# A second buffer for transposed attention blocks, laid over the space of the layer normalisation

## What is computed

```
def _cross_attention(q_in, kv_in, ...):
    qh = (q_in @ wq + bq).reshape(b, q_len, H, K)
    kh = (kv_in @ wk + bk).reshape(b, t, H, K)
    vh = (kv_in @ wv + bv).reshape(b, t, H, K)
    kh = concatenate([kh, bias_k], axis=1)      # one learned row more
    vh = concatenate([vh, bias_v], axis=1)
    weights = softmax(einsum('bqhk,bthk->bhqt', qh, kh) / sqrt(K))
    ctx = einsum('bhqt,bthk->bqhk', weights, vh).reshape(b, q_len, H * K)
    return ctx @ wo + bo

x = x + cross_attention(layer_norm(x), context)     # layer 1
x = x + cross_attention(layer_norm(x), context)     # layer 2
x = x + gelu(layer_norm(x) @ w_fc1 + b_fc1) @ w_fc2 + b_fc2
```

## Time and profile before

| | us |
|---|---|
| median of three runs | 630.03 |
| the profiled execution | 630.57 |
| its span, first to last instruction | 628.8 |
| TensorE busy | 527.1 (84%) |
| VectorE busy | 417.3 (66%) |
| GpSimd busy | 391.0 (62%) |
| ScalarE busy | 341.7 (54%) |
| mean granted clock of TensorE, share of full speed | 0.964 |

### The profile page before, as it was taken

The page is one execution under the profiler, slowest core; times in us unless marked ns, Lnnn a source line. Parts: engine busy times, 40 slices in busy tenths (PEclk is TensorE's granted clock), DMA queues, the critical chain, the costliest instruction groups (busy, mean ns, idle before and its releaser), DMA issues.

```text
span 628.8 us, 10915 instructions
## 1 busy us (share of the span) xinstructions
PE 527.1 (84%) x3217; PEld 456.6 (73%) x3217; DVE 417.3 (66%) x864; ACT 341.7 (54%) x715; POOL 391.0 (62%) x358
## 2 busy tenths in 40 slices
PE   7985888879696989889984896979889897968787
PEld 5865767768585868778863785868777776858787
DVE  3967657575767677665785557677675757566684
ACT  3463746556464847465364464748375655647422
POOL 3736648485857668485744658667584858575830
PEclk9987999999999989899988899999899999999889
DMA  7323424352433434240403533434343424320100
GB/s 230 101 67 76 122 72 121 75 138 67 119 98 79 117 75 121 72 123 13 88 18 75 130 80 104 102 75 121 75 121 75 129 67 135 82 71 15 35 0 35
DMA packets 47909, 55.31 MB, mean 88 GB/s; under 512 B 8698, under 2 KB 33422, under 8 KB 47886
## 3 DMA queue, kind: packets, MB, share of 16 engines
q1 hardware_dynamic: 47886, 55.03, 33.6%
HBM read 25.11 MB, written 0.52 MB: 41 GB/s over the span
## 4 chain that ended last, share of the span: by engine, by line
SPq 39%; DVE 18%; PE 14%; DMA 10%; issue 10%; ACT 5%; POOL 1%; DVEq 0%; ACTq 0%; POOLq 0%
SPq L246 39%; PE ring L998 8%; DVE blocks L727 8%; DMA wf_lo<-blocks 5%; DMA wf_hi<-blocks 4%; ACT probs L557 4%; PE acc L998 3%; DVE total L764 3%; DVE row_max L755 2%; DVE v_sum L712 1%; POOL probs L372 1%; PE ps_ctx L998 1%; DVE z_sb L791 1%; DMA probs<-ctx_in 1%; DVE o_lo L748 1%
## 5 line engine op out<-in xcount | busy, mean ns | idle before, releaser
L365 POOL TENSOR_TENSOR v_lo<-v_sum,v_hi 128x512 fp32r<-128x512 f32 x64 | 85.4, 1337 | 67.7 <-ACT v_hi L515 67.6
L727 DVE STREAM_TRANSPOSE blocks<-probs 128x512 f32<-128x512 f32 x112 | 72.2, 685 | 81.8 <-DMA wf_hi<-blocks 81.8
L557 ACT ACTIVATE probs<-ring,shift 128x512 f32<-128x512 f32 x112 | 76.0, 679 | 52.4 <-DVE shift L760 52.4
L998 PE MATMUL ring<-k_lo,q_hi 128*128 128x512 f32 x112 | 48.2, 431 | 39.7 <-DVE k_lo L697 34.8
L998 PE MATMUL ring<-pT_lo,v_hi 128*128 128x256 f32 x240 | 70.0, 292 | 8.0 <-DVE v_sum L712 8.0
L755 DVE TENSOR_REDUCE row_max<-ring 128x1 f32<-128x512 f32 x112 | 74.2, 681 | 3.3 <-PE ring L998 3.2
L377 POOL TENSOR_TENSOR pT_lo<-wf_lo,pT_hi 128x1024 fp32r<-128x1024 f32 x28 | 67.3, 2404 | 6.5 <-ACT pT_hi L532 6.4
L764 DVE TENSOR_TENSOR total<-row_sum,p_learned 128x2 f32<-128x2 f32 x64 | 31.0, 484 | 59.8 <-ACT probs L557 59.6
L998 PE MATMUL ring<-pT_hi,v_lo 128*128 128x256 f32 x240 | 68.5, 285 | 0.0
L998 PE MATMUL ring<-pT_hi,v_hi 128*128 128x256 f32 x240 | 68.0, 283 | 0.0
L515 ACT ACTIVATE v_hi<-v_sum 128x512 fp32r<-128x512 f32 x64 | 40.1, 629 | 43.2 <-DVE v_sum L712 43.2
(11 more groups left out here) (170 smaller groups left out, 1717.5 us busy)
## 6 DMA issues: line engine op xcount, KB each, us to landing
wf_hi<-blocks SPq DMA_DIRECT2D x224, 64.0 KB, 2.0
wf_lo<-blocks SPq DMA_DIRECT2D x224, 64.0 KB, 2.0
wk_raw<-wk_in SPq DMA_DIRECT2D x17, 256.0 KB, 5.9
wq_raw<-wq_in SPq DMA_DIRECT2D x17, 256.0 KB, 3.0
wv_raw<-wv_in SPq DMA_DIRECT2D x16, 256.0 KB, 3.1
vrows<-vrows_in SPq DMA_DIRECT2D x16, 256.0 KB, 6.2
wo_raw<-wo_in SPq DMA_DIRECT2D x16, 256.0 KB, 6.0
wf_raw<-wf_in SPq DMA_DIRECT2D x6, 256.0 KB, 2.7
```

Source lines behind the costliest of these rows:

```text
L365: pool.tensor_tensor(v_lo[:, 2 * m:2 * m + 2, :], v_sum[:, m % 2, :].rearrange("p (t c) -> p t c", c=PW), v_hi[:, 2 * m:2 * m + 2, :].bitc ...
L557: act.activation(probs[:, u, q, :], ring[S_BANKS[where][QTB * u + q]][:], ACT.Exp, bias=shift[:, u, q:q + 1], scale=SCALE, accum_out=row_s ...
L727: last = dve.transpose(blocks[:, :, u % 2, :, q, :].rearrange("p g c b -> p c g b"), probs[:, u, q, :].rearrange("p (c g b) -> p c g b", g ...
L998: ins = pe.matmul(out_ap, a, b, start=start and i == 0, stop=stop and i == len(passes) - 1)
```

## The change

`z_sb` and `h_full` become two views of one tile, `norm_space`. `blocks` becomes a list of two buffers of 8 KB: a tile of its own for units 0 and 1, and the whole of `norm_space` for units 2 and 3. `move` reads the buffer of its batch. `transpose_blocks` writes the buffer of its batch and waits for the landing of the same move of the step before; in the first step of layer 1 (the first that the kernel runs) it does not wait for a landing at all. No instruction is added or taken away on any engine, and their order stays.

```diff
-        z_sb = sb("z_sb", [P, QT, D])
-        h_full = sb("h_full", [P, DC, TOK])
+        norm_space = sb("norm_space", [P, QT * D + DC * TOK])
+        z_sb = norm_space[:, 0:QT * D].rearrange("p (t d) -> p t d", d=D)
+        h_full = norm_space[:, QT * D:QT * D + DC * TOK].rearrange("p (c t) -> p c t", c=DC)
...
-        blocks = sb("blocks", [P, QB, 2, CTB, QTB, BLK])
+        blocks = [space.rearrange("p (g u c q b) -> p g u c q b", g=QB, u=2, c=CTB, q=QTB)
+                  for space in (sb("block_space", [P, QB * RUN])[:], norm_space[:])]
...
                         sp.dma_start(moved_to[n][BLK * g:BLK * (g + 1), i, :],
-                                     blocks[BLK * i:BLK * (i + 1), g, :, :, :, :].rearrange("p u c q b -> p (u c q b)")).then_inc(landed[n], LOAD)
+                                     blocks[n][BLK * i:BLK * (i + 1), g, :, :, :, :].rearrange("p u c q b -> p (u c q b)")).then_inc(landed[n], LOAD)
...
                 done = pair - layer
-                if u < 2:
-                    if not first or layer > 0:
-                        dve.wait_ge(landed[1], QB * QB * LOAD * done)
-                else:
-                    dve.wait_ge(landed[0], QB * QB * LOAD * (done + 1))
+                if not first or layer > 0:
+                    dve.wait_ge(landed[u // 2], QB * QB * LOAD * done)
                 dve.wait_ge(p_ready_act, NU * pair + (u + 1 if u != 2 else 2))
                 dve.wait_ge(p_ready_pool, NU * pair + (u + 1 if u < 2 else NU))
                 for q in range(QTB):
-                    last = dve.transpose(blocks[:, :, u % 2, :, q, :].rearrange("p g c b -> p c g b"),
+                    last = dve.transpose(blocks[u // 2][:, :, u % 2, :, q, :].rearrange("p g c b -> p c g b"),
                                          probs[:, u, q, :].rearrange("p (c g b) -> p c g b", g=QB, b=BLK))
                 last.then_inc(blocks_ready, 1)
```

## The result

The changed kernel takes 591.82 us (median of four runs, 589.86 to 593.36), the kernel before 629.85 us in the same comparison: ratio 0.9394, interval 0.9363 to 0.9425. That is 38 us less; 594.0 was forecast. The profiled execution of the changed kernel took 593.36 us, the slowest of its four; its span is 591.6 us, 37.2 us less than before.

What follows compares the result with a forecast made beforehand. No engine was full; the prediction blamed the second move waiting for the first's landing through a shared buffer. Gains of 18.0 us per layer, 36.0 in all, took 630.57 to 594.6, median 594.0; likeliest case 589 to 601, 8-in-10 range 584 to 610.

Steps and rivals of the forecast that it cites:

- The wait removed: Transposes of units 2 and 3 end near 186.4, so the second move starts near 187.7 and lands 4.3 us earlier.
- limit of 0.3: Sign in the profile after: the 32 DMAs of line 246 run without a gap over 0.3 us between the moves.
- The second landing becomes slack: Steady step: of the second landing's 4.3 us, 1.8 end as slack; the step gains 2.5, becoming 32.1 us.
- The meeting of VectorE and GpSimd: VectorE's pT_lo of unit 1 is held by GpSimd's, so the next v_sum comes 1.2 us earlier, not 1.8.
- GpSimd's run, then scores, then maximum: Steady step: wo_lo ends 1.2 us earlier, and VectorE's maximum of unit 2, waiting for TensorE's scores, starts 2.5 us earlier.
- The sum: Per layer 3.4 (first interval) + 12.5 (five steady) + 2.1 (last step) = 18.0 us; two layers 36.0.
- First intervals: First interval of each layer, without value work: gain taken as 3.4 us, between 2.5 and 4.0.
- Last steps: Last step of each layer: TensorE's output of unit 1 comes earlier by 1.2 + 0.9 = 2.1 us.
- (a): Rival: GpSimd's chain is shorter or the two pT_lo do not exclude each other; step gains 3.0, time 587; chance 0.20.
- (b): Rival: the 128x2 addition of unit 1 stays late behind GpSimd's pT_lo; step gains 1.1, time 609; chance 0.18.
- (c): Rival: transposes of units 2 and 3 or the second move held by something else; no gain, 630 us; chance 0.03.
- (d): Rival: SP's queue cannot take 32 DMAs at 0.63 us each; slower, 675 at 1.1 us each; chance 0.04.

Runs made afterwards that it cites:

- run with the small remainder: Changed kernel with VectorE making only 64 of the 1024 columns of unit 1's remainder (pT_lo), the rest left out: 579.36 us, ratio 0.9187.
- runs with wo first: GpSimd splits wo ahead of wk: in the changed kernel 577.13 us (ratio 0.9152), in the kernel before 630.17 us (ratio 0.9997).
- own-tile run: Changed kernel with the second buffer in a tile of its own instead of the layer normalisation's space: 591.64 us, ratio 0.9378.
- first experiment: Changed kernel keeping both buffers, but with the transposes waiting for the landings as in the kernel before: 630.37 us, ratio 1.0008.

## Why the prediction was right

**The wait removed.** Foreseen: the transposes end while move 0 is still being issued, and move 1 starts right behind it. They end at 176.23, the issuing at 177.17. The gap left is 0.33 us, slightly more than the 0.1 that was allowed for, and at the limit of 0.3 that was named as a sign. (The two moves are 20.0 of 34.6 us, 58% of a step and not two thirds; nothing rests on it.)

**The second landing becomes slack.** Foreseen with a gain of 4.3 us for the landing and 2.5 for the step. ScalarE's rounding at 189.03 has no idle time before it: the landing (177.50 + 10.00 + 1.5 = 189.0) and o_hi (188.68 + 0.47) came together, as forecast. The addition was forecast to be through right after wo_lo; it is held by GpSimd's wo_lo itself and ends with it, at 192.42. The two runs with extra DMAs show the slack. This holds for the steady steps. For the move of a layer's first step the landing is not slack on ScalarE, which waits 2.36 and 2.90 us for it.

**The meeting of VectorE and GpSimd.** Forecast for VectorE's pT_lo: held until GpSimd's is through, over 1.5 us. It takes 1.67 to 1.97 us in all 14 places, and the run with the small remainder shows the holding by itself. The next v_sum comes 15.99 us after the step's first DMA instead of 17.25, 1.26 earlier (1.2 forecast). By the rule of the Trainium skill ("SBUF — State Buffer", section Who interferes with whom) it is the order of issue that decides who waits, not the size of the instruction. The traces agree: VectorE's instructions of 1024, 64 and 2 columns were all held when GpSimd's had been issued first, the last by 0.15 us.

**GpSimd's run, then scores, then maximum.** wo_lo ends 25.27 us into the step (26.50 before), the maximum starts at 27.06 (29.70 before): 1.2 and 2.6 us, against 1.2 and 2.5 forecast. The pair of runs with wo first shows the link as a cause, since one order is worth 15 us in one kernel and nothing in the other. This too is shown for the steady steps.

**The sum.** Steady: 2.62 and 2.65 us each against 2.5. First intervals: 3.06 and 2.97 us against 3.4, and here the reason was wrong as well. The forecast lay between 4.0 from the landing and 2.5 if GpSimd's run holds, and took the two missing v_lo as what decides. wo_lo was ready over 4 us before the maximum in both first intervals; what came last was the addition, issued behind GpSimd's pT_lo and held to its end. In the own-tile run, with the landing on time in layer two, it was held as well, and the interval gained 3.94 us (2.66 in layer one). Last steps: 2.60 and 2.67 against 2.1. In layer one TensorE's output of unit 1 comes 2.24 us earlier (260.05 - 231.05 = 29.00 us after the last move 0, 31.24 before), close to forecast, and a further 0.4 us comes behind it; the granted clock of that later stretch is 0.97 before and 1.00 after. In layer two the output comes 2.58 us earlier (31.58 to 29.00; before, it waited 1.21 us for o_lo there, and not 0.88) and only 0.1 us comes behind it, at a clock of 0.94 in both. That fits the clock as the source of the 0.4, but was not tested. In all 36.0 forecast and 37.2 measured in the profiled executions: the steady and last steps gave 2.4 us more than forecast, the first intervals 0.8 less, and the start to the first move was 0.45 longer. These misses partly cancel in the total, which is luck; the median (591.82) is 2.2 us below the 594.0.

**The rivals.** (a) would have had pT_lo at 1.22 us and a step below 31.7; it is 1.71 and 31.95. (The prediction gives the gain of a step in that case once as 3.1 and once as 3.0 us.) (b), the late addition, was not met in the steady intervals, but it was met in the first one of each layer; its working gave these a gain of 2.9 us, and 3.06 and 2.97 were measured. The run with four extra DMAs made it happen in the steady steps at its price: 33.3 us a step, where the working of (b) gives 34.6 - 1.1 = 33.5. (c) fell with the first experiment. (d), a queue that cannot take 32 DMAs at their pace, did not come: the median issue is 590 ns as before, and landing takes 2.0 us in the median.

## What to carry to other kernels

A buffer that two transfers share makes the second wait until the first has landed (here a gap of 4.4 us a step), but freeing it pays only up to the next chain that starts from something unchanged (here 2.6 of the 4.4): follow each chain from the first event that does not move (here the landing of move 0) and take the smallest gain. Follow them again for the steps at the ends of a loop, where other work is missing: here the first interval had another last chain than the steady ones. Where VectorE reads two operands from SBUF beside GpSimd, read the ends of both rows: a short instruction that ends with the other engine's long one is waiting for it, and its slack has an edge. After such a change, look again at orders that did not matter before; a swap of two weight splits that was worth nothing gave 15 us.

## What the runs showed of the hardware

Single issues can be long. In the changed kernel move 1 of the first step took 11.26 us of issuing instead of 10.0, and the longest single issue of line 248 is 1829 ns at a median of 590, with one landing of 3.7 us. Before it was 1495 ns and 2.9 us. It happens in few places and its cause stays open. In the changed kernel the long issue of layer one and the long landing of layer two both belong to the move of a first step, for which ScalarE waits; how much time they cost there no run shows. The block transposes, 128x512 in fp32 from SBUF to SBUF, never waited for GpSimd: 667 to 705 ns in all 112 of the changed kernel, although GpSimd's instructions ran beside many of them.
